# Moving the Vector engine's preparation of later weights from the projections of the first layer to the copies of its product stage

## The chip, the cores and the metric

The kernel runs on one core of a Trainium2 chip, in one launch. The metric is the device time of that launch in microseconds, median of several runs. One execution was profiled; all times inside the kernel are of that execution, counted from the start of its span. Engines are TensorE (PE, with its weight loads as PEld), the Vector engine (DVE), the Scalar engine (ACT), GpSimd (POOL) and SyncE (SP), which issues the DMAs.

## The reference, cut to what matters

The input `x` is an array of 128 x 128 positions with 32 channels. Eight layers follow each other, each added to its input. Four are mixers: a triangle product (L0), another (L1), a recurrent convolution over rows (SC) and a third triangle product (L3). Between them stand a top-k expert layer (F0), two sigmoid recurrences (R1 and R2) and a top-2 expert layer (F3). The change works in L0:

```
zn  = layernorm(x)
a   = sigmoid(zn @ Wga + bga) * (zn @ Wla + bla)
b   = sigmoid(zn @ Wgb + bgb) * (zn @ Wlb + blb)
k   = einsum('bimc,bmjc->bijc', a, b)          # per channel a 128 x 128 product
out = sigmoid(zn @ Wgo + bgo) * (layernorm(k) @ Wlo + blo)
x   = x + out
```

L1 and L3 have the same form, with the second operand of the product the other way round. The weights of L1, L3, F0, R1 and R2 must be scaled and laid out in blocks on the chip before their layers use them.

## The kernel before

All of `x` stays in on-chip memory. Its 128 x 4096 floats are worked on in 32 blocks `s` of 128 columns (4 rows of the picture by 32 channels), or in 8 batches `b` of 4 blocks. Each engine has its own program written out by hand, in order, and they meet on counting semaphores. DVE runs the layer norm of L0, then `tri_dve` for L0, then `f0_dve`, and so on.

A triangle layer goes through these stages:

- **Projection**, 32 blocks. TensorE multiplies block `s` by the projection weights (line 504) into one of four PSUM slots. ACT takes two sigmoids from the slot, `gate` (line 579) and `sig` (line 583). DVE multiplies the linear part by `sig` into `ab` (line 645) and signals `lin`. TensorE may not project block `s` before `lin` has been signalled for block `s - 4`, since it reuses that slot.
- **Turn**, L0 alone, 8 batches. TensorE transposes the second operand (line 364) into PSUM banks 0 and 1 in turn. ACT copies the even batches to `z_t` (line 372), DVE the odd ones (line 370). TensorE waits before batch `b` for the copy of batch `b - 2`.
- **Product**, 8 batches. TensorE makes the per-channel products (line 534) in four banks. ACT copies the even batches to `z` (line 573), DVE the odd ones (line 571, in `k_copy`). Before batch `b` of 4 or more TensorE waits for the copy of batch `b - 4`. The odd batches of the product also wait for DVE's copies of the turn, batch for batch.
- **Output**, 8 batches. When all product copies are done TensorE transposes `z` (line 555) and projects it (line 545). ACT squares, DVE sums, inverts and gates (lines 662, 668, 674), POOL scales and adds (lines 711, 716). The layer norm of the next layer is interleaved here.

While this goes on POOL copies weights of the convolution into `toep` (line 1209), and then forms the additive part of the output, two instructions for each of 8 batches (lines 621 and 630). It needs these before the output stage.

In L0's projection stage DVE also prepares weights of later layers, through the dictionary `between` of `tri_dve`, before blocks 4, 8, 12, 16 and 20:

- before blocks 4 and 8, `tri_weights1_dve` for L1 and L3: four instructions each (lines 451, 452, 453, 456);
- before blocks 12 and 16, `rec_weights1_dve` for R1 and R2: two instructions each (line 980), each from two operands in on-chip memory;
- before block 20, `f0_weights_dve`: two instructions (line 767).

TensorE reads the F0 weights when `f0_pe` begins, after all of L0, and the other four sets in `later_weights_pe`, in the middle of F0.

Of the kernel before, what the change touches and what calls it, by code (L numbers as in the profile page):

```python
# [107 lines left out]
def build(nc, x_d, par_d, row_d, mask_d, w1_d, w2_d, w2l_d, out_d):  # L108
    with ExitStack() as ctx:
# [47 lines left out]
        def bank(b, cols=BANK, n=1):  # L157
            return PSUM[:, b * BANK:b * BANK + (n - 1) * BANK + cols]
# [4 lines left out]
        def pcol(name, rows=GC):  # L163
            a, n = PAR[name]
            return par[0:rows, a:a + n]
# [48 lines left out]
        def wait_all(eng, levels):  # L214
            for s, v in levels:
                eng.wait_ge(s, v)

        t0 = stage("L0", "norm weights ones tri", "bt_ps bt_act bt_dve", src=XC, scratch=XR, eps=0, e2=EPS)
        f0 = stage("F0", "norm turn", "w_dve lg_ps lg_act pad best top neg cand_ps cand fin mk_ps mk sel exp esum tot_ps tot w wt_ps"
                   " wt_act wt_dve pool_ps pl plt_ps plt h_ps h o_ps outm_ps outm y_ps done", src=XC, eps=1, e2=0.0)  # L220
        t1 = stage("L1", "norm weights ones tri", "ab", src=XC, scratch=XR, eps=0, e2=EPS)
        r1 = stage("R1", "norm turn rec", "g_ps g_y0 g_y1 g_edge_ps g_edge g_turned", src=XC, eps=1, e2=0.0)
# [4 lines left out]
        r2 = stage("R2", "norm turn rec", "g_ps g_y0 g_y1 g_edge_ps g_edge g_turned", src=XC, eps=1, e2=0.0)  # L227
        t3 = stage("L3", "norm weights ones tri", src=XC, scratch=XR, eps=0, e2=EPS)
# [138 lines left out]
        def turn_copy(eng, L, b, dst, done, ps="zt_ps"):  # L367
            eng.wait_ge(L.s[ps], L.at[ps] + b + 1)
            if b % 2:
                eng.tensor_copy(dst, bank(b % 2)).then_inc(L.s[done], 1)  # L370
            else:
                eng.activation(dst, bank(b % 2), ACT.Copy).then_inc(L.s[done], 1)
# [76 lines left out]
        def tri_weights1_dve(dve, L):  # L449
            l, sm = L.name, L.s["w_half"]  # L450
            dve.tensor_scalar(scaled[l][:, :], pcol(f"{l}_w"), pcol(f"{l}_lnw"), None, ALU.mult).then_inc(sm, 1)
            dve.tensor_scalar(wotmp[l][:, GC:], pcol(f"{l}_wo"), pcol(f"{l}_low"), None, ALU.mult).then_inc(sm, 1)
            dve.tensor_scalar(lnb_at[l][:, :], last[:, :, :].rearrange("p g c -> p (g c)"), pcol(f"{l}_lnb", C), None,
                              ALU.mult).then_inc(sm, 1)
            dve.wait_ge(sm, L.at["w_half"] + 2)
            dve.tensor_tensor(wotmp[l][:, 0:GC].rearrange("p (g c) -> p g c", g=G),
                              wotmp[l][:, GC:].unsqueeze(1).to_broadcast([GC, G, C]),
                              m4[:, :].unsqueeze(2).to_broadcast([GC, G, C]), ALU.mult).then_inc(sm, 1)
# [106 lines left out]
        def k_copy(eng, L, b):  # L565

            eng.wait_ge(L.s["k_ps"], L.at["k_ps"] + b + 1)
            out = Z[:, :].rearrange("p (s g c) -> p c g s", g=G, c=C)[:, 4 * b:4 * b + 4]
            src = bank(KB[b % 4]).rearrange("p (c g s) -> p c g s", c=4, g=G)
            if b % 2:  # L570
                eng.tensor_copy(out, src).then_inc(L.s["k_dve"], 1)
            else:
                eng.activation(out, src, ACT.Copy).then_inc(L.s["k_act"], 1)
# [56 lines left out]
            eng.tensor_tensor(x, x, blocks(L.src)[:, :, 4 * b:4 * b + 4, :].rearrange("p g s c -> p s g c"), ALU.add)\  # L630
                .then_inc(L.s["xb"], 1)

        def tri_dve(dve, L, after, between={}):
            for s in range(S):
                if s in between:
                    between[s](dve)
                dve.wait_ge(L.s["sig"], L.at["sig"] + s + 1)
                sig = SIG[:, s % SLOTS, :].rearrange("p (h g w) -> p h g w", h=2, g=2)
                if L is t1:
                    if s >= 2:  # L640
                        dve.wait_ge(L.s["ab"], L.at["ab"] + s - 1)
                    dst = TMP[:, s % 2, 0:2 * GC].rearrange("p (h g w) -> p h g w", h=2, g=2)
                else:
                    dst = to_ab(s).rearrange("p (h g) w -> p h g w", h=2)
                dve.tensor_tensor(dst, slot(s)[:, :, :, 2 * C:4 * C], sig, ALU.mult).then_inc(L.s["lin"], 1)  # L645
                if L is t1 and s % 4 == 2 and s > 4:
                    gate_bias(dve, L, s // 4 - 1)
                    if s > 8:
                        add_x(dve, L, s // 4 - 2)
            if L is t1:  # L650
                gate_bias(dve, L, S // 4 - 1)
                add_x(dve, L, S // 4 - 2)
                add_x(dve, L, S // 4 - 1)
            if L is t0:
                for b in range(1, C // 4, 2):
                    turn_copy(dve, L, b, BT[:, 4 * b:4 * b + 4, :], "bt_dve", "bt_ps")
            for b in range(1, C // 4, 2):
                k_copy(dve, L, b)

            def out_sum(b):  # L660
                dve.wait_ge(L.s["o_sq"], L.at["o_sq"] + b + 1)
                dve.tensor_reduce(stats[:, 2, 16 * b:16 * b + 16],
                                  SQR[:, b * BANK:(b + 1) * BANK].rearrange("p (n c) -> p n c", c=C), AX.X, ALU.add)\
                    .then_inc(L.s["o_sum"], 1)

            def out_inverse(b):
                dve.wait_ge(L.s["o_std"], L.at["o_std"] + b + 1)
                dve.reciprocal(stats[:, 3, 16 * b:16 * b + 16], stats[:, 0, 16 * b:16 * b + 16]).then_inc(L.s["o_rstd"], 1)  # L668

            def out_gate(b):  # L670
                dve.wait_ge(L.s["o_rg"], L.at["o_rg"] + b + 1)
                if b >= 2:
                    dve.wait_ge(L.s["done"], L.at["done"] + b - 1)
                dve.tensor_tensor(TMP[:, b % 2, 0:BANK].rearrange("p (s h f) -> p h s f", s=4, h=2),  # L674
                                  o_bank(b)[:, :, :, 0, :],
                                  GATE[:, b * BANK:(b + 1) * BANK].rearrange("p (s h f) -> p h s f", s=4, h=2), ALU.mult)\
                    .then_inc(L.s["o_mul"], 1)

            for t in range(TRI_LN + LN_STEPS if after else S // 4 + 4):
                if 4 <= t < S // 4 + 4:  # L680
                    out_gate(t - 4)
                if 3 <= t < S // 4 + 3:
                    out_inverse(t - 3)
                if 2 <= t < S // 4 + 2:
                    out_sum(t - 2)
                if after:
                    ln_dve_step(dve, after, t - TRI_LN)
# [76 lines left out]
        def f0_weights_dve(dve):  # L764
            v = gw[:, :, :].rearrange("p q (b r e) -> p q b r e", b=G, r=2)
            for q in range(2):
                dve.tensor_tensor(v[:, q, :, q, :], pcol("gate").unsqueeze(1).to_broadcast([GC, G, E0]),
                                  m4[:, :].unsqueeze(2).to_broadcast([GC, G, E0]), ALU.mult).then_inc(f0.s["w_dve"], 1)
# [208 lines left out]
        def rec_weights1_dve(dve, L):  # L977
            W = rec_w[L.name]
            for name, key in (("W", "wbd"), ("VT", "vt")):
                dve.tensor_tensor(W[key][:, :].rearrange("p (g c) -> p g c", g=G),  # L980
                                  pcol(f"{L.name}_{name}").unsqueeze(1).to_broadcast([GC, G, C]),
                                  m4[:, :].unsqueeze(2).to_broadcast([GC, G, C]), ALU.mult).then_inc(L.s["w_half"], 1)
# [636 lines left out]
        @block.vector  # L1619
        def _(dve):  # L1620
            consts_dve(dve)
            ln_dve_step(dve, t0, 0)
            dve.wait_ge(par_first, PAR_FIRST)
            tri_weights1_dve(dve, t0)
            for u in range(1, LN_STEPS):
                ln_dve_step(dve, t0, u)
                if u == 1:
                    tri_weights2_dve(dve, t0)

            tri_dve(dve, t0, f0, {  # L1630
                4: lambda dve: tri_weights1_dve(dve, t1), 8: lambda dve: tri_weights1_dve(dve, t3), 12: lambda dve: rec_weights1_dve(dve, r1),
                16: lambda dve: rec_weights1_dve(dve, r2), 20: f0_weights_dve})
            f0_dve(dve)
            tri_dve(dve, t1, r1)
            rec_dve(dve, r1, None)
            turn_x_copy(dve, v1, 1)
            ln_dve(dve, sc)
            scan_dve(dve)
            turn_x_copy(dve, v2, 1)
            ln_dve(dve, r2)  # L1640
            rec_dve(dve, r2, t3)
            tri_dve(dve, t3, f3)
            f3_dve(dve)
# [73 lines left out]
```

## Time and profile before

| | |
|---|---|
| median of 3 runs | 615.32 us (614.03 to 616.44) |
| the profiled execution | 615.61 us |
| its span, first to last instruction | 613.8 us |
| PE busy | 455.4 us (74%) |
| DVE busy | 383.7 us (63%) |
| ACT busy | 237.9 us (39%) |
| POOL busy | 249.5 us (41%) |
| mean granted TensorE clock | 0.842 of full speed |
| chain that ended last | PE 54%, DVE 31%, ACT 6% |

The span and 1.81 us around it make the time of the profiled execution. L0's projection, turn and product stages lie between 28 and 64 us, less than a tenth of the span. The chain that ended last is followed back from the last instruction, step by step, to what released each instruction; only work on it can shorten the time.

### The profile page before, as it was taken

What the parts mean: (1) busy time and instruction counts of PE and PEld (TensorE: products, weight loads), DVE (VectorE), ACT (ScalarE), POOL (GpSimd) and SP (SyncE); (2) the same over time, 40 slices, a digit from 0 to 9 for tenths busy, and PEclk for the clock granted to TensorE, in tenths of its full rate; (3) what the DMA queues carried; (4) which work ended last, traced back from release to release, by engine and by line L of the source; (5) the groups of instructions that cost most, each with busy time, mean ns of one, the idle gap of its engine ahead of it and who ended that gap; (6) DMA issues with size and microseconds to landing.
All of it is one profiled execution on the core that took longest, in us unless ns stands there. A gap on an engine that the chain in (4) does not pass through costs nothing.

```text
span 613.8 us, 8600 instructions
## 1 busy us (share of the span) xinstructions
PE 455.4 (74%) x3018; PEld 356.4 (58%) x3018; DVE 383.7 (63%) x1148; ACT 237.9 (39%) x573; POOL 249.5 (41%) x325
## 2 busy tenths in 40 slices
PE   3788738798575854699658994879769854926996
PEld 2457634677342843399638994469636743914664
DVE  5796595535868487600792448920579489098885
ACT  1576534301465452457351003547449653200000
POOL 2795485000477078200050000500058478117995
PEclk9999967587789895989858999879859995557999
DMA  9100000000000000000000000000000000000323
GB/s 176 44 2 1 1 1 1 0 2 0 0 2 1 1 1 1 1 2 1 1 1 1 1 1 1 1 1 2 1 1 3 1 0 2 0 0 1 50 38 51
DMA packets 34105, 6.02 MB, mean 10 GB/s; under 512 B 33644, under 2 KB 33772, under 8 KB 34029
## 3 DMA queue, kind: packets, MB, share of 16 engines
q1 hardware_dynamic: 34062, 5.46, 5.1%
q8 instruction: 25, 0.41, 0.3%
q14 instruction: 18, 0.15, 0.1%
HBM read 3.36 MB, written 2.10 MB: 9 GB/s over the span
## 4 chain that ended last, share of the span: by engine, by line
PE 54%; DVE 31%; ACT 6%; issue 3%; POOL 3%; DMA 1%; SPq 1%; DVEq 0%; POOLq 0%
PE psum L1242 6%; DVE moments L290 6%; DVE ab L645 5%; PE psum L1003 5%; PE psum L504 5%; PE psum L384 5%; PE psum L1002 5%; DVE z L298 4%; PE psum L534 4%; PE psum L1415 3%; PE psum L545 3%; PE psum L1024 2%; PE psum L1393 2%; ACT z_t L319 2%; PE psum L1435 2%
## 5 line engine op out<-in xcount | busy, mean ns | idle before, releaser
L330 POOL TENSOR_TENSOR z<-z,stats 128x496 f32<-128x496 f32 (+1 forms) x64 | 67.0, 1047 | 136.6 <-DVE z L298 136.6
L384 PE MATMUL psum<-ident,z 128*128 128x128 f32 x256 | 57.6, 371 | 39.6 <-POOL z L330 38.4
L384 PEld LDWEIGHTS psum<-ident,z 128*128 128x128 f32 x256 | 41.3, 191 | 68.6 <-POOL z L330 48.3
L504 PE MATMUL psum<-wp_L,z_t 64*128 64x320 f32 x384 | 65.0, 477 | 11.1 <-DVE tmp L645 6.2
L319 ACT ACTIVATE z_t<-psum 128x512 f32<-128x512 f32 x56 | 40.1, 721 | 67.3 <-PE psum L384 67.3
L290 DVE BATCH_NORM_STATS2 moments<-x_cols 128x6 f32<-128x64 f32 x448 | 61.9, 210 | 2.1 <-POOL x_cols L716 1.7
L504 PEld LDWEIGHTS psum<-wp_L,z_t 64*128 64x128 f32 x384 | 37.3, 198 | 33.9 <-issue 27.4
L327 POOL MEMSET z<- 128x16 f32 x32 | 4.0, 125 | 128.1 <-DVE z L298 128.1
L1095 ACT ACTIVATE ab<-psum,mv 128x128 f32<-128x128 f32 x112 | 41.3, 369 | 19.9 <-PE psum L1003 9.5
L1003 PE MATMUL psum<-ab,R_vt 128*128 128x128 f32 x224 | 48.8, 302 | 0.0
L1002 PE MATMUL psum<-z_t,wbnt 128*128 128x128 f32 x224 | 46.6, 292 | 0.8 <-DVE wbnt L1148 0.8
L298 DVE TENSOR_TENSOR z<-x_cols,moments 128x496 f32<-128x496 f32 (+1 forms) x56 | 46.9, 838 | 0.0
L545 PE MATMUL psum<-wo_L,z_t 64*128 64x128 f32 x384 | 30.6, 303 | 20.7 <-DVE tmp L674 20.0
L711 POOL TENSOR_TENSOR gate<-gate,stats 128x512 f32<-128x512 f32 x24 | 25.1, 1048 | 45.4 <-DVE stats L668 45.2
L1522 POOL TENSOR_TENSOR z<-gate 128x512 f32<-128x512 f32 x31 | 38.7, 1267 | 7.0 <-DVE gate L1496 6.9
L1242 PE MATMUL psum<-ab,toep 128*128 128x128 f32 x336 | 39.4, 280 | 2.5 <-POOL ab L1225 1.6
L545 PEld LDWEIGHTS psum<-wo_L,z_t 64*128 64x128 f32 x384 | 26.2, 204 | 25.4 <-issue 14.2
L1242 PEld LDWEIGHTS psum<-ab,toep 128*128 128x128 f32 x336 | 39.1, 195 | 3.1 <-issue 3.1
L1496 DVE TENSOR_TENSOR gate<-psum,ab 128x1024 f32<-128x1024 f32 x32 | 37.8, 1219 | 4.4 <-PE psum L1420 3.3
L307 ACT ACTIVATE stats<-moments,eps 128x16 f32<-128x16 f32 x64 | 19.6, 307 | 50.1 <-DVE moments L290 50.1
L645 DVE TENSOR_TENSOR ab<-psum,sig 128x256 f32<-128x256 f32 x64 | 33.3, 604 | 7.8 <-ACT sig L583 7.8
L1002 PEld LDWEIGHTS psum<-z_t,wbnt 128*128 128x128 f32 x224 | 36.9, 207 | 1.4 <-DVE wbnt L1148 1.4
(244 smaller groups left out, 934.7 us busy)
## 6 DMA issues: line engine op xcount, KB each, us to landing
x_cols<-in_x_dram SPq DMA_DIRECT2D x16, 128.0 KB, 2.9
out_dram<-x_cols SPq DMA_DIRECT2D x32, 64.0 KB, 1.9
par<-in_par_dram SPq DMA_DIRECT2D x1, 644.5 KB
w<-in_w_dram SPq DMA_DIRECT2D x1, 264.0 KB
w<-in_w_dram SPq DMA_DIRECT2D x1, 256.0 KB
mask<-in_mask_dram SPq DMA_DIRECT2D x1, 64.0 KB
row<-in_row_dram SPq DMA_DIRECT2D x1, 3.3 KB
w2l<-in_w2l_dram SPq DMA_DIRECT2D x1, 2.0 KB
```

Source lines behind the costliest of these rows:

```text
L290: m = dve.bn_stats(moments[:, q, k:k + 2, :].rearrange("p k m -> p (k m)"), X4[:, SQ * q + s, g:g + 2, :].rearrange("p g c -> p c g"))
L298: dve.tensor_tensor(Z4[:, r, :, 0:c], X4[:, r, :, 0:c], ln_moment(before, 1).unsqueeze(3).to_broadcast([N, SQ, G, c]), ALU.subtract)\
L319: act.activation(dst, bank(q % 2).rearrange("p (s n) -> p s n", s=4), ACT.Copy).then_inc(L.s["zt"], 1)
L330: pool.tensor_tensor(Z4[:, r, :, 0:c], Z4[:, r, :, 0:c], RSTD[:, q].unsqueeze(3).to_broadcast([N, SQ, G, c]), ALU.mult).then_inc(L.s["z"], 1)
L384: m = pe.transpose(bank(b % 2)[:, k * N:(k + 1) * N], block_of(Z)(4 * b + k), ident[:, :])
L504: m = pe.matmul(bank(slot_bank(s) + h, 2 * 5 * C), ZT[rows, s, :], wp[l][rows, :, :], start=True, stop=True)
L545: m = pe.matmul(o_bank(b)[:, h, k, :, :], ZT[rows, 4 * b + k, :], wo[l][rows, :, rows], start=True, stop=True)
L645: dve.tensor_tensor(dst, slot(s)[:, :, :, 2 * C:4 * C], sig, ALU.mult).then_inc(L.s["lin"], 1)
L1002: return (pe.matmul(o, W["wbnt"][:, :], chunks(ZTIME, off, h), start=True, stop=False), lambda: pe.matmul(o, W["vt"][:, :], chunks(Y, off, ...
L1003: lambda: pe.matmul(o, W["vt"][:, :], chunks(Y, off, h), start=False, stop=True))
L1095: act.activation(chunks(Y, first + k + 1, h), bank(2 * h + k % 2, NS), ACT.Sigmoid, bias=bias).then_inc(L.s[f"step_y{h}"], 1)
L1242: m = pe.matmul(bank(2 + h, ROWS_S * NB), toep[:, b, :, :], scan_rows(SCN[:, :, b:b + NB], off, h), start=(b == 0), stop=(b == 2))
```

## The change

The dictionary goes, with its hook in the block loop. The same five calls are made later in L0's `tri_dve`, between the copies: L1's weights after the turn's copy 5, L3's after copy 7, R1's after the product's copy 1, R2's after its copy 3, F0's after its copy 7. The instructions are the same and in the same order among themselves. No wait and no semaphore is changed, no DMA is touched, and the other engines' programs stay as they are.

```diff
-        def tri_dve(dve, L, after, between={}):
+        def tri_dve(dve, L, after):
             for s in range(S):
-                if s in between:
-                    between[s](dve)
                 dve.wait_ge(L.s["sig"], L.at["sig"] + s + 1)
...
             if L is t0:
                 for b in range(1, C // 4, 2):
                     turn_copy(dve, L, b, BT[:, 4 * b:4 * b + 4, :], "bt_dve", "bt_ps")
+                    if b == 5:
+                        tri_weights1_dve(dve, t1)
+                tri_weights1_dve(dve, t3)
             for b in range(1, C // 4, 2):
                 k_copy(dve, L, b)
+                if L is t0 and b == 1:
+                    rec_weights1_dve(dve, r1)
+                if L is t0 and b == 3:
+                    rec_weights1_dve(dve, r2)
+            if L is t0:
+                f0_weights_dve(dve)
...
-            tri_dve(dve, t0, f0, {
-                4: lambda dve: tri_weights1_dve(dve, t1), 8: lambda dve: tri_weights1_dve(dve, t3), 12: lambda dve: rec_weights1_dve(dve, r1),
-                16: lambda dve: rec_weights1_dve(dve, r2), 20: f0_weights_dve})
+            tri_dve(dve, t0, f0)
```

## Rows read from the trace of the kernel before

**Rows 1.** Chain that ended last, L0: start us, us, engine, output, line.

```profile
29.09 1.94 DVE ab L645 x4
...
36.83 1.27 DVE R_vt L980
...
45.56 4.42 DVE ab L645 x8
...
55.44 7.16 PE psum L534 x64
62.63 1.02 DVE z L571
```

**Rows 2.** Timeline of DVE, L0's projection: start us, us, ..., idle before and releaser.

```profile
30.89 0.27 DVE L451 TENSOR_SCALAR scaled_L<-par 128x160 f32<-128x160 f32 x1
...
31.62 1.91 DVE L645 TENSOR_TENSOR ab<-psum,sig 128x256 f32<-128x256 f32 x4
...
35.92 0.92 DVE L980 TENSOR_TENSOR R_wbd<-par,m 128x128 f32<-128x128 f32 x1
36.76 1.35 DVE L980 TENSOR_TENSOR R_vt<-par,m 128x128 f32<-128x128 f32 x1
38.03 1.93 DVE L645 TENSOR_TENSOR ab<-psum,sig 128x256 f32<-128x256 f32 x4
39.80 0.88 DVE L980 TENSOR_TENSOR R_wbd<-par,m 128x128 f32<-128x128 f32 x1
40.61 0.28 DVE L980 TENSOR_TENSOR R_vt<-par,m 128x128 f32<-128x128 f32 x1
40.81 1.94 DVE L645 TENSOR_TENSOR ab<-psum,sig 128x256 f32<-128x256 f32 x4
42.60 0.87 DVE L767 TENSOR_TENSOR gw<-par,m 128x64 f32<-128x64 f32 x2
43.39 1.94 DVE L645 TENSOR_TENSOR ab<-psum,sig 128x256 f32<-128x256 f32 x4
45.56 4.41 DVE L645 TENSOR_TENSOR ab<-psum,sig 128x256 f32<-128x256 f32 x8 [0.23 <-ACT sig L583]
```

**Rows 3.** Timeline of DVE, L3's projection.

```profile
460.99 1.95 DVE L645 TENSOR_TENSOR ab<-psum,sig 128x256 f32<-128x256 f32 x4 [4.34 <-ACT sig L583]
463.16 15.36 DVE L645 TENSOR_TENSOR ab<-psum,sig 128x256 f32<-128x256 f32 x28 [0.21 <-ACT sig L583]
```

**Rows 4.** Timeline of PE, projections of L0 and L3 from block 4 on.

```profile
29.84 7.44 PE L504 MATMUL psum<-wp_L,z_t 64*128 64x320 f32 x48 [0.36 <-DVE ab L645]
...
461.73 15.58 PE L504 MATMUL psum<-wp_L,z_t 64*128 64x320 f32 x112 [0.35 <-DVE ab L645]
```

**Rows 5.** Timeline of DVE, L0's turn, product and start of output.

```profile
54.04 0.69 DVE L370 COPY z_t<-psum 128x512 f32<-128x512 f32 x1 [0.75 <-PE psum L364]
...
57.27 1.05 DVE L571 COPY z<-psum 128x512 f32<-128x512 f32 x1 [1.09 <-PE psum L534]
59.05 1.04 DVE L571 COPY z<-psum 128x512 f32<-128x512 f32 x1 [0.74 <-PE psum L534]
...
66.94 0.69 DVE L662 TENSOR_REDUCE stats<-squares 128x16 f32<-128x512 f32 x1 [3.30 <-ACT squares L594]
```

**Rows 6.** Timeline of POOL beside them.

```profile
36.64 1.31 POOL L621 TENSOR_TENSOR x_rows<-gate,bo_L 128x512 f32<-128x512 f32 x1
...
53.67 1.27 POOL L630 TENSOR_TENSOR x_rows<-x_rows,x_cols 128x512 f32<-128x512 f32 x1
```

**Rows 7.** Timeline of PE in F0, the same eight matmuls twice.

```profile
123.34 3.60 PE L801 MATMUL psum<-z,gate 128*128 128x256 f32 x8
...
127.21 1.89 PE L801 MATMUL psum<-z,gate 128*128 128x256 f32 x8
```

**Rows 8.** Stretches in F0: us, busy by engine, PEclk (granted clock), DMA.

```profile
124.00:125.00 1.00, 1.00 (x4) 0.82 (x3) 0.22 (x2) 0.00 (x0) 0.00 (x0) 0.50 0.00 0
...
127.00:128.00 1.00, 1.00 (x8) 0.92 (x7) 0.00 (x0) 0.59 (x1) 0.00 (x0) 1.00 0.00 0
```

## The prediction

> **What bounds the kernel now.** I read the page's shares first: TensorE is busy for 74% of the span, DVE for 63%. Those are means over unlike stages, so I went to the chain of waits in L0, where the change acts. The reader is to see in it [rows 1] that between 29.09 and 49.98 us nearly every piece is DVE's: multiplications of line 645, and between them weight instructions such as `R_vt`. So in this stage the weight instructions lie on the path that sets the end. Further on the chain goes to TensorE's products (line 534, 7.16 us) and then to DVE's last product copy.
>
> The second view is DVE's timeline over the same stretch [rows 2]. Four multiplications start to start take 1.80 us (29.09 in the chain [rows 1] to 30.89), or 0.45 each, and DVE has no idle time until 45.56, where it waits for ACT for the first time; from there eight take 4.41 us, 0.54 each. DVE alone could run at 0.45, something else at 0.54, and the weight work is what keeps DVE behind until just before 45.56.
>
> The third view is the same stage in L3, which has no weight work between its blocks [rows 3]. It is the same line, shape and count. There 32 multiplications go from 460.99 to 478.52, 17.53 us. TensorE's timeline says what sets that pace [rows 4]: its 112 records for 28 blocks fill 15.58 us with no wait shown inside, 0.556 a block, while in L0 the first 12 of these blocks (48 records) took 7.44 us and so 0.62 a block. So without the weights TensorE's projections and the loop over the four slots bound the stage, at L3's pace.
>
> **What is removed.** Fourteen instructions in five groups leave the projection stage. Start of the group to the multiplication behind it [rows 2]: L1's four 31.62 - 30.89 = 0.73, L3's four the same pattern, 0.73, R1's two 38.03 - 35.92 = 2.11, R2's two 40.81 - 39.80 = 1.01, F0's two 43.39 - 42.60 = 0.79. Sum 5.37 us. Check: 24 multiplications at 0.45 are 10.8; 29.09 + 10.8 + 5.37 = 45.3, where DVE does catch up. The saving is not 5.37, because TensorE then holds DVE back. I take the size from L3: L0's stage now takes 45.56 + 4.41 - 29.09 = 20.88 us, L3's 17.53. **Saving: 20.88 - 17.53 = 3.35 us.** The ends: at most 5.37 if nothing else held DVE, which L3 excludes; at least 3.0 if TensorE ran a little slower than in L3 (28 blocks at 0.567, which would add 0.3). I take 3.35: same instructions, and both stages run with POOL at work beside them.
>
> **What is added, group by group.** The turn and product stages move 3.35 us earlier as a whole; their inner gaps stay. I give the old times.
>
> L1's group goes behind the turn's copy 5, which starts at 54.04 and ends at 54.73. The copies there wait 0.75 us for TensorE each time [rows 5], and the group takes 0.73: hidden, with nothing to spare. What is queued behind it is copy 7. The product batch that reads copy 7 is the last one, and it starts at 55.44 + 7 x 0.895 = 61.7, so some 5 us of lateness would be borne there.
>
> L3's group goes behind copy 7. Before the first product copy DVE is idle for 1.09 us [rows 5]; the group takes 0.73: hidden, 0.36 to spare. Behind it is product copy 1, which TensorE needs at batch 5, at 55.44 + 5 x 0.895 = 59.9. The copy now ends at 58.32, so 1.6 us late costs nothing there.
>
> R1's and R2's groups go behind product copies 1 and 3, into gaps of 0.74 us [rows 5]. What they cost depends on POOL. In the projection stage the four instructions of line 980 took 0.92, 1.35, 0.88 and 0.28 us, all the same shape [rows 2]. The 1.35 us one starts at 36.76 and ends at 38.11; POOL's line 621 runs from 36.64 to 37.95 [rows 6], so it ended just behind POOL's. Undisturbed, the shape takes 0.28, and start to start 0.20 (40.61 to 40.81). Where are these groups against POOL? POOL is back to back and its schedule does not depend on this change; it ends at 53.67 + 1.27 = 54.94. R1's group now starts at 58.3 - 3.35 = 54.97. So it comes just as POOL ends: 0.40 us, hidden in 0.74. R2's is well clear. If R1's still took 2.11, copy 3 would start 1.37 late; TensorE needs it at batch 7 (61.7), it now ends at 60.09, so 1.6 us of cover remains, and the next gaps win 0.74 and more back.
>
> F0's group goes behind the last product copy. DVE then has 3.30 us idle [rows 5], against 0.79. TensorE wants these weights only after L0.
>
> The Trainium skill, "SBUF — State Buffer", section "Who interferes with whom", speaks against the change here: a Vector instruction with two on-chip inputs, or a `tensor_scalar` in a two-port mode, and a GpSimd instruction that reads the same memory exclude each other, and the later one fully blocks. The trace agrees for line 980 (1.35 us against 0.28). By the rule all eight instructions of the L1 and L3 groups, now moved from beside POOL's short `toep` copies to beside its long instructions, could each be held for one of these.
>
> Its price from rows: the first of these groups now starts at 54.73 - 3.35 = 51.4 and POOL runs to 54.9, so all the holds together are at most 3.5 us. Suppose DVE stands still until 54.9 and only then does the first group (0.73), copy 7 (0.69), the second group (0.73): these end at 57.1 and copy 1 at 58.1, where TensorE needs it at 59.9 - 3.35 = 56.55. TensorE stalls 1.5 us, and DVE, with 0.40 of R weights and 1.04 of copy in each 1.78 us from one copy's start to the next (57.27 to 59.05), follows again. So the added side costs **0 to 1.5 us**. I take 0: a hold of one POOL instruction (1.3 us) fits into 0.36 + 1.6.
>
> **Sum.** -3.35 + 0 = -3.35. The profiled execution, 613.8 span and 1.81 around it, would go from 615.61 to 612.26, the span to 610.45. That execution is 0.29 over the median of 615.32, so the median becomes **612.0 us** (-0.54%). POOL's end at 54.9 is no new bound: its next work is in the output stage, behind the last product copy, which starts at 62.63 and so at 59.28. Everything after L0 hangs on its end and on no DMA.
>
> **TensorE's clock** can add to it or take from it. The same eight matmuls of F0 take 3.60 us where the granted clock is 0.50 (1.2 GHz) and 1.89 where it is 1.00 (2.4 GHz) [rows 7, 8]. If a change of level falls one such batch earlier or later relative to the work, that is 1.7 us either way. I put nothing for it into the sum and use it for the range.
>
> **The rivals.** My forecast, 612.0, has 0.68; its own range is 610.3 to 613.7 by the 1.7 us.
>
> *POOL holds the moved groups.* As worked out: stall 1.5 us, gain 1.85, 613.5. For it is the 1.35 us row; against it the cover of 1.6 us. Chance 0.13.
>
> *The gain is given back or never comes.* L0 would not reach L3's pace, or the levels of TensorE's clock fall two batches of 1.7 us worse behind L0, which takes the whole 3.35: 615.3. For it: changes of level are there and F0 is bound by TensorE. Against: L3 shows the pace. Chance 0.11.
>
> *Faster still*: a clock change falls two batches better: 608.6. Chance 0.04.
>
> *Slower: the copies of the product become DVE's bound.* Twelve moved instructions stand ahead of the last product copy, on which the output stage waits. The idle time there is 0.75 + 1.09 + 3 x 0.74 = 4.06 us. If each were held as the worst row shows (1.35), they cost 16.2 - 4.06 = 12.1, net +8.8, 624.1. It decides the sign from a mean of (4.06 + 3.35) / 12 = 0.62 us an instruction, and is slower by over 0.5% from 0.87. Against it: POOL is done at 54.9, before the four R instructions, and no more than 3.5 us of holding is to be had. Chance 0.04.
>
> **How the numbers follow.** About 0.5% (3.08 us) is what a measurement of this kernel can tell from no change, so faster means below 612.24. My forecast lies 0.27 below that bound: of its 0.68 I count 0.41 as faster and 0.27 as the same. With 0.04 from the case faster still and 0.02 of the first rival (where the hold is short) that is 0.47 faster; slower is 0.04; the rest, 0.49, is the same. The range of 609.9 to 614.4 holds the forecast's own range and the first rival, 0.81, and leaves out the ends.
>
> **What would show it.** In the changed kernel's profile the multiplications of line 645 in L0 should stand without weight instructions between them and take 17.5 us, TensorE's 28 blocks 15.6. DVE's idle time before the copies should shrink from 0.75, 1.09 and 0.74 to about 0, 0.36 and 0.34, and that before the first `squares` sum from 3.30 to about 2.5. TensorE's products should still take 7.16 us with no wait for DVE. The R1 instructions should take 0.28 each. The prediction is wrong if product copies 1 or 7 start late and the chain runs over weight instructions again, or if the output stage starts 3.35 us earlier but the end does not: then the clock's stretches will have changed.

## The result and the profile after

The changed kernel takes 612.5 us (median of 12 runs, 611.12 to 614.04), the kernel before 615.85 us in the runs made beside it (614.03 to 617.55). The ratio is 0.9946, with a 95% interval of 0.9931 to 0.996: 0.54% less, 3.35 us. The forecast was 612.0 us and -0.54%. The profiled execution took 612.13 us with a span of 610.4, where the sum had 612.26 and 610.45.

DVE's timeline through L0, rows as in [rows 2] and [rows 5]:

```profile
29.23 1.95 DVE L643 TENSOR_TENSOR ab<-psum,sig 128x256 f32<-128x256 f32 x4 [3.06 <-ACT sig L583]
31.39 15.34 DVE L643 TENSOR_TENSOR ab<-psum,sig 128x256 f32<-128x256 f32 x28 [0.22 <-ACT sig L583]
...
50.80 0.69 DVE L370 COPY z_t<-psum 128x512 f32<-128x512 f32 x1 [0.75 <-PE psum L364]
51.41 0.46 DVE L451 TENSOR_SCALAR scaled_L<-par 128x160 f32<-128x160 f32 x1
51.79 1.25 DVE L452 TENSOR_SCALAR wotmp_L<-par 128x32 f32<-128x32 f32 x1
...
53.35 0.67 DVE L370 COPY z_t<-psum 128x512 f32<-128x512 f32 x1
53.95 0.71 DVE L451 TENSOR_SCALAR scaled_L<-par 128x160 f32<-128x160 f32 x1
...
55.13 1.03 DVE L571 COPY z<-psum 128x512 f32<-128x512 f32 x1
56.01 0.27 DVE L987 TENSOR_TENSOR R_wbd<-par,m 128x128 f32<-128x128 f32 x1
...
56.40 1.02 DVE L571 COPY z<-psum 128x512 f32<-128x512 f32 x1
...
59.38 1.01 DVE L571 COPY z<-psum 128x512 f32<-128x512 f32 x1 [0.69 <-PE psum L534]
60.25 0.33 DVE L774 TENSOR_TENSOR gw<-par,m 128x64 f32<-128x64 f32 x2
63.69 0.69 DVE L669 TENSOR_REDUCE stats<-squares 128x16 f32<-128x512 f32 x1 [3.11 <-ACT squares L594]
```

The multiplications now stand together, from 29.23 to 46.73: 17.50 us, where they took 20.88 [rows 1, 2] and L3's take 17.53 [rows 3]. The moved groups fill the time in which DVE waited for TensorE. Two instructions stand out, at 51.79 and 53.95, far longer than their like before. In the kernel before the one of line 452 was

```profile
31.08 0.23 DVE L452 TENSOR_SCALAR wotmp_L<-par 128x32 f32<-128x32 f32 x1
```

and the one of line 451 took 0.27 us [rows 2].

TensorE's timeline of the same stages, to be read beside [rows 4]:

```profile
29.96 15.55 PE L504 MATMUL psum<-wp_L,z_t 64*128 64x320 f32 x112 [0.35 <-DVE ab L643]
...
52.03 7.31 PE L534 MATMUL psum<-ab,z_t 128*128 128x128 f32 x64
60.54 1.06 PE L555 MATMUL psum<-ident,z 128*128 128x128 f32 x8 [1.20 <-DVE z L571]
```

Its 28 blocks run without a wait (15.55 us), its products too (7.31, as before), and the output stage begins 1.20 us after them. Before the change the wait was the same 1.20 us, and the stage began at 63.79, 3.25 us later:

```profile
63.79 1.06 PE L555 MATMUL psum<-ident,z 128*128 128x128 f32 x8 [1.20 <-DVE z L571]
```

From the start of the output stage to the end of the span it is 550.0 us before (613.8 - 63.79) and 549.9 after (610.4 - 60.54), so in these two executions nothing behind L0's product stage changed. POOL's timeline:

```profile
51.72 1.28 POOL L621 TENSOR_TENSOR x_rows<-gate,bo_L 128x512 f32<-128x512 f32 x1
53.08 1.48 POOL L630 TENSOR_TENSOR x_rows<-x_rows,x_cols 128x512 f32<-128x512 f32 x1
```

The chain that ended last, in order of time, has no weight instruction between the first multiplication and the output stage:

```profile
31.39 15.35 DVE ab L643 x28
...
50.80 0.70 DVE z_t L370
...
52.20 7.16 PE psum L534 x64
...
59.38 1.02 DVE z L571
```

### The profile page after: what moved, and what is told of

Read it like the earlier page. It is cut to its first block, busy times and chain, and to the rows that moved or that the text cites. A ratio compares the mean times of both kernels' runs of the same rounds, so it can differ in the third digit from the quotient of the medians.

```text
span 610.4 us, 8600 instructions
## 1 busy us (share of the span) xinstructions
PE 453.6 (74%) x3018; PEld 354.2 (58%) x3018; DVE 384.0 (63%) x1148; ACT 237.5 (39%) x573; POOL 249.0 (41%) x325
## 4 chain that ended last, share of the span: by engine, by line
PE 54%; DVE 31%; ACT 6%; issue 3%; POOL 3%; DMA 1%; SPq 1%; DVEq 0%; POOLq 0%
PE psum L1249 6%; DVE moments L290 6%; DVE ab L643 5%; PE psum L1010 5%; PE psum L1009 5%; PE psum L384 5%; DVE z L298 4%; PE psum L504 4%; PE psum L534 4%; PE psum L1422 3%; PE psum L545 3%; PE psum L1031 2%; PE psum L1400 2%; ACT z_t L319 2%; PE psum L1442 2%
## 5 line engine op out<-in xcount | busy, mean ns | idle before, releaser
L504 PEld LDWEIGHTS psum<-wp_L,z_t 64*128 64x128 f32 x384 | 35.6, 197 | 32.2 <-issue 27.3
L643 DVE TENSOR_TENSOR ab<-psum,sig 128x256 f32<-128x256 f32 x64 | 34.6, 607 | 7.8 <-ACT sig L583 7.8
```

The costliest lines, as they stand in the source:

```text
L504: m = pe.matmul(bank(slot_bank(s) + h, 2 * 5 * C), ZT[rows, s, :], wp[l][rows, :, :], start=True, stop=True)
```

## The experiments

Unless said otherwise each median is of 10 to 12 runs, and the kernel before ran beside them: 615.69 us for the first four, 616.42 for the next ones. Their intervals are 0.32% to 0.51% wide, so a time is good to about 1 us, and stage lengths are taken from profiles. Outside of the stages at issue the executions differ by as much: in the 13 profiles the first multiplication starts between 28.2 and 29.2 us, and from the start of L0's output stage to the end it is 549.2 to 550.8 us, in one case 551.9. In 5 of the 13 profiles of this study (with those of before and after) TensorE's granted clock is 0.50, that is 1.2 GHz, for some 3 us from about 29 or 30 us. Here is that stretch in the first experiment, windows with granted clock third from the end:

```profile
26.00:30.00 4.00, 2.93 (x15) 1.48 (x15) 1.41 (x4) 3.03 (x11) 3.88 (x20) 0.81 0.01 2
30.00:31.00 1.00, 1.00 (x6) 0.74 (x4) 0.53 (x2) 0.20 (x2) 0.94 (x7) 0.50 0.00 0
```

A projection stage with this stretch is compared only with another such.

**All five groups behind the last product copy.**

```diff
             for b in range(1, C // 4, 2):
                 k_copy(dve, L, b)
...
             if L is t0:
+                tri_weights1_dve(dve, t1)
+                tri_weights1_dve(dve, t3)
+                rec_weights1_dve(dve, r1)
+                rec_weights1_dve(dve, r2)
                 f0_weights_dve(dve)
```

> The changed kernel with all five weight groups behind the last product copy, where DVE is idle 3.11 us in the changed kernel; unheld they need 0.73 + 0.73 + 0.40 + 0.40 + 0.2 = 2.5 us. Theory (in the changed kernel the copies that start up to 1.2 us late are fully covered by the four product banks): product copies now start on time, and nothing is gained: output stage starts as long after the first multiplication as in the changed kernel (31.3 us), median within 0.3 us of its 612.5. Rival (the late copies or POOL's 1.48 us instruction cost something hidden): faster than the changed kernel by 0.5 to 1.5 us.

Measured: 612.48 us, ratio 0.9947 (0.9929 to 0.9965), the same as the changed kernel. DVE's timeline:

```profile
54.68 1.04 DVE L571 COPY z<-psum 128x512 f32<-128x512 f32 x1 [1.10 <-PE psum L534]
56.46 1.04 DVE L571 COPY z<-psum 128x512 f32<-128x512 f32 x1 [0.74 <-PE psum L534]
...
64.35 0.69 DVE L666 TENSOR_REDUCE stats<-squares 128x16 f32<-128x512 f32 x1 [0.81 <-ACT squares L594]
```

The copies are on time, all groups fit before the first sum of squares with 0.81 us to spare, and nothing is gained by it. So the late copies of the changed kernel cost nothing that these runs can tell. (From first multiplication to output stage it takes 32.6 us and not 31.3, because this profile has the stretch at 1.2 GHz: its projection stage is 18.79 us long.)

**L1's and L3's groups back in the projection.**

```diff
             for s in range(S):
+                if L is t0 and s == 4:
+                    tri_weights1_dve(dve, t1)
+                if L is t0 and s == 8:
+                    tri_weights1_dve(dve, t3)
                 dve.wait_ge(L.s["sig"], L.at["sig"] + s + 1)
...
-                    if b == 5:
-                        tri_weights1_dve(dve, t1)
-                tri_weights1_dve(dve, t3)
```

> The changed kernel with the L1 and L3 groups (four instructions each) back before blocks 4 and 8 of the projection; the R1, R2 and F0 groups stay moved. Theory (TensorE loses what DVE is late beyond the slots' slack): in the kernel before TensorE's first 12 waiting blocks took 7.44 us, 0.77 more than at L3's pace, so these two groups cost 0.8 us of their 1.46; projection stage 18.3 us, median 613.3. Rival A (their debt is paid back in full by DVE's surplus of 0.1 us a block): 17.5 us, 612.5. Rival B (each us of DVE work costs a us): 19.0 us, 614.0.

Measured: 613.39 us, ratio 0.9957 (0.9938 to 0.9975). The median is where the theory has it, 0.9 over the changed kernel, but rival B's 614.0 is not excluded by it. The profile has the stretch at 1.2 GHz, and its stage, 29.10 to 49.95, takes 20.85 us. Against the 18.79 of the first experiment, which has that stretch too, this is 2.06 us more, where the theory had 0.8 and rival B 1.5. In this execution one instruction of a group was held:

```profile
35.39 1.29 DVE L453 TENSOR_SCALAR lnb_at_L<-last,par 32x128 f32<-32x128 f32 x1
```

This had been 0.27 us in the kernel before, so about 1 of the 2.06 us is this hold. What the two groups cost in the stage at full clock no run shows. POOL's line 630 stands beside it:

```profile
35.30 1.30 POOL L630 TENSOR_TENSOR x_rows<-x_rows,x_cols 128x512 f32<-128x512 f32 x1
```

**The kernel before, with POOL late.** Only POOL's start on the additive part is moved, so that no long POOL instruction runs beside a weight group. The weight groups stay in the projection.

```diff
                 pool.wait_ge(L.s["w_dve"], L.at["w_dve"] + TRI_W)
+                if L is t0:
+                    pool.wait_ge(L.s["lin"], L.at["lin"] + 22)
                 for b in range(S // 4):
                     gate_bias(pool, L, b)
```

> The kernel before, weight groups inside the projection, but POOL starts its additive part of L0's output only after 22 of the 32 multiplications, so none of its long instructions runs beside a weight group. POOL then ends near 62 us, before the output stage needs it. Theory (more than half of the 5.37 us of the groups was DVE held by POOL): the line 980 instructions take 0.28 us each, the groups sum to about 2.5 us, the projection stage takes 18.4 us (20.9 before), median 613.3. Rival (the price is the count of the instructions, the holds matter little): stage 20.2 us or more, median 615.2. Rival (line 980 is slow for another reason, such as fetching its code): it stays at 0.9 to 1.35 us.

Measured: 612.94 us, ratio 0.9936 (0.9915 to 0.9956): POOL's start alone is worth what the change is worth, as far as the runs can tell (the two medians differ by 2.75 us, which is at the edge of that interval). The first profile has the stretch at 1.2 GHz and a stage of 20.03 us, 1.24 over the first experiment's 18.79. A second profile of the same kernel:

> The kernel before with POOL's late start once more, for a profile: in the first one TensorE's granted clock was 0.50 from about 30 to 33 us, which lengthened the projection stage (20.0 us). Theory: where the clock stays at 1.00 in that stretch the stage takes 18.4 us. Rival (the groups still cost nearly what they did): 20 us at full clock too.

One execution, 612.91 us, with full clock throughout the stage. DVE's timeline, beside [rows 2]:

```profile
35.89 0.26 DVE L982 TENSOR_TENSOR R_wbd<-par,m 128x128 f32<-128x128 f32 x1
36.08 0.27 DVE L982 TENSOR_TENSOR R_vt<-par,m 128x128 f32<-128x128 f32 x1
36.28 2.22 DVE L645 TENSOR_TENSOR ab<-psum,sig 128x256 f32<-128x256 f32 x4
...
40.53 0.34 DVE L769 TENSOR_TENSOR gw<-par,m 128x64 f32<-128x64 f32 x2
40.91 6.59 DVE L645 TENSOR_TENSOR ab<-psum,sig 128x256 f32<-128x256 f32 x12
```

Line 980's instructions (here 982) take 0.26 to 0.28 us, R1's group 0.39 and not 2.11. The stage runs from 29.08 to 40.91 + 6.59 = 47.50: 18.42 us, as expected; neither rival has that. The five groups now take 2.65 us together (0.74, 0.75, 0.39, 0.39 and 0.38), in place of 5.37. So of the 3.38 us that the weights cost in the projection, 20.88 - 18.42 = 2.46 were POOL's holds, and 18.42 - 17.50 = 0.92 is what was left of the groups' own 2.65.

**The changed kernel, with POOL late.** The same edit in the changed kernel.

> The changed kernel with POOL's start as late as in the run above: POOL now runs beside all of the turn and product stages. It ends near 62 us, and the output stage needs it at 66. Theory (POOL holds DVE instructions with two on-chip inputs and tensor_scalar; the cover of the product copies is finite, some 1.6 us to TensorE's batches 5 and 7, and none behind the last copy): R1's and R2's groups are held too (1 to 2 us each instead of 0.4), product copy 3 starts over 2 us late, TensorE stalls and the last copy is late: slower than the changed kernel by 0.5 to 2.5 us. Rival (holds are absorbed whatever they are): same as the changed kernel, last copy on time.

Measured: 615.63 us, ratio 0.9998 (0.998 to 1.0016): the whole gain is gone, 3.1 us, more than the 0.5 to 2.5 expected. DVE's timeline:

```profile
53.64 1.25 DVE L452 TENSOR_SCALAR wotmp_L<-par 128x32 f32<-128x32 f32 x1
...
56.08 0.49 DVE L989 TENSOR_TENSOR R_wbd<-par,m 128x128 f32<-128x128 f32 x1
56.49 1.35 DVE L989 TENSOR_TENSOR R_vt<-par,m 128x128 f32<-128x128 f32 x1
57.77 1.03 DVE L571 COPY z<-psum 128x512 f32<-128x512 f32 x1
58.65 0.54 DVE L989 TENSOR_TENSOR R_wbd<-par,m 128x128 f32<-128x128 f32 x1
59.11 1.36 DVE L989 TENSOR_TENSOR R_vt<-par,m 128x128 f32<-128x128 f32 x1
60.39 1.88 DVE L571 COPY z<-psum 128x512 f32<-128x512 f32 x2
```

and TensorE's:

```profile
56.37 2.02 PE L534 MATMUL psum<-ab,z_t 128*128 128x128 f32 x16 [0.78 <-DVE z L571]
58.94 1.13 PE L534 MATMUL psum<-ab,z_t 128*128 128x128 f32 x8 [0.55 <-DVE z L571]
62.42 1.06 PE L555 MATMUL psum<-ident,z 128*128 128x128 f32 x8 [2.35 <-DVE z L571]
63.73 2.08 PE L545 MATMUL psum<-wo_L,z_t 64*128 64x128 f32 x16 [0.25 <-ACT z_t L605]
```

The projection stage is as short as in the changed kernel (17.49 us). But all four of R1's and R2's instructions are held now, TensorE waits 0.78 and 0.55 for copies 1 and 3, and 2.35 for the last, in place of 1.20. The output stage starts 62.42 - 28.16 = 34.26 us after the first multiplication, against 31.31: 2.95 later. After these waits the granted clock falls to 0.50 (1.2 GHz) shortly before 64 us, which the expectation did not count: the first output projection takes 2.08 us, not 1.16, and the first sum of squares comes 38.33 us after the first multiplication, 3.87 later than in the changed kernel.

**R1's and R2's groups back in the projection.**

```diff
             for s in range(S):
+                if L is t0 and s == 12:
+                    rec_weights1_dve(dve, r1)
+                if L is t0 and s == 16:
+                    rec_weights1_dve(dve, r2)
                 dve.wait_ge(L.s["sig"], L.at["sig"] + s + 1)
...
-                if L is t0 and b == 1:
-                    rec_weights1_dve(dve, r1)
-                if L is t0 and b == 3:
-                    rec_weights1_dve(dve, r2)
```

> The changed kernel with the R1 and R2 groups (two instructions of line 980 each) back before blocks 12 and 16 of the projection, POOL at its usual place; the L1, L3 and F0 groups stay moved. Theory (POOL's holds make these four instructions the dear ones: 2.11 and 1.01 us in the kernel before, where TensorE then waited 1.48 and 0.37): projection stage about 19.5 us, median 614.5, 2.0 over the changed kernel, dearer than the eight instructions of the L1 and L3 groups were (0.9). Rival (price goes by count and length, 4 x 0.20 = 0.8 us, most of it absorbed): stage 17.7, median 612.7.

Measured: 613.64 us, ratio 0.9958 (0.9942 to 0.9974). That is 2.8 under the kernel before and so some 0.6 over the changed one, not 2.0; the rival's figure is nearer. Its profile has the stretch at 1.2 GHz, and the four instructions took 0.49, 0.28, 0.81 and 0.28 us. A second profile of the same kernel:

> R1 and R2 groups inside the projection, once more for a profile. In the first profile their four instructions took 0.49, 0.28, 0.81 and 0.28 us, 1.56 us start to next multiplication for both groups, not 3.12. Theory (how long POOL holds them depends on where in a POOL instruction they come, and that moves with the stretch of granted clock 0.50 near 30 us): without that stretch the groups cost another sum, above 2 us, and the stage takes over 18.5 us. Rival (they cost 1.6 us wherever nothing was late before them): again 1.5 to 1.7.

One execution, full clock in the stage:

```profile
35.43 0.74 DVE L987 TENSOR_TENSOR R_wbd<-par,m 128x128 f32<-128x128 f32 x1
36.09 1.35 DVE L987 TENSOR_TENSOR R_vt<-par,m 128x128 f32<-128x128 f32 x1
37.36 1.93 DVE L647 TENSOR_TENSOR ab<-psum,sig 128x256 f32<-128x256 f32 x4
39.15 0.88 DVE L987 TENSOR_TENSOR R_wbd<-par,m 128x128 f32<-128x128 f32 x1
...
42.31 6.60 DVE L647 TENSOR_TENSOR ab<-psum,sig 128x256 f32<-128x256 f32 x12 [0.22 <-ACT sig L583]
```

The groups take 1.93 and 1.00 us and the stage 42.31 + 6.60 - 28.99 = 19.92, 2.42 over the changed kernel. In the execution with the slower stretch it took 20.12 against 18.79 in the first experiment, 1.33 over. The mechanism is as the theory has it; its size goes by the execution, and the median shows less of it (some 0.6) than either profile does. Why the median shows so little stays open. In the execution with the slower stretch the stage is 2.62 us longer than in the changed kernel's profile and the whole only 1.43 (613.56 against 612.13): it started its multiplications 0.81 us sooner and took 0.4 us less behind the product stage.

**A load behind product copy 5, and the same behind copy 7.** Ten instructions whose result nobody reads are added, into a new tile `spare`, with `b == 5` in one kernel and `b == 7` in the other:

```diff
                 if L is t0 and b == 3:
                     rec_weights1_dve(dve, r2)
+                if L is t0 and b == 5:
+                    for k in range(10):
+                        dve.tensor_tensor(spare[:, k, :], cent[:, :], ident[:, :], ALU.mult)
```

> The changed kernel with ten extra instructions that nobody reads (128x128, two on-chip inputs, 0.20 us each, 2.0 in all) behind product copy 5 of L0, when POOL is idle. Theory (the last product copy is the one without cover): DVE ends copy 5 at 58.55 and the load at 60.55, copy 7 was due at 59.38, so it is 1.2 late and so is everything behind it: median 613.7. Rival (the wait on the last copy is hidden by ACT's copy or the output's fill): within 0.3 of 612.5.

> The same ten extra instructions behind product copy 7, where DVE is idle 3.11 us in the changed kernel. Theory: hidden, the first sum of squares is on time, median 612.5. Rival (any DVE work in L0 costs its length): 614.5.

Measured, beside 616.42 for the kernel before: 614.20 us (ratio 0.9959, 0.9943 to 0.9976) behind copy 5, and 613.25 us (7 runs, ratio 0.9932, 0.9906 to 0.9957) behind copy 7. Taken as differences to the kernel before on the same chip these are -2.2 and -3.2, against the changed kernel's -3.35: by the medians the load costs 1.1 us in the one place and next to nothing in the other. The intervals overlap, so the profiles have to carry this. DVE's and TensorE's rows for the load behind copy 5:

```profile
58.24 2.08 DVE L667 TENSOR_TENSOR spare<-cent,ident 128x128 f32<-128x128 f32 x10
60.25 0.99 DVE L572 COPY z<-psum 128x512 f32<-128x512 f32 x1
...
61.39 1.92 PE L556 MATMUL psum<-ident,z 128*128 128x128 f32 x8 [2.31 <-DVE z L572]
```

TensorE waits 2.31 us for the last copy in place of 1.20, which is 1.11 more. In this execution more is lost behind it, for the granted clock (third from the end) falls:

```profile
62.00:63.00 1.00, 1.00 (x7) 0.90 (x5) 0.00 (x0) 0.51 (x1) 0.00 (x0) 0.50 0.00 0
```

The eight transposes take 1.92 us, not 1.06, and the first sum of squares comes 36.89 us after the first multiplication, 2.43 later than in the changed kernel. Behind copy 7 the load leaves the first sum of squares 1.10 us to spare:

```profile
61.38 2.08 DVE L667 TENSOR_TENSOR spare<-cent,ident 128x128 f32<-128x128 f32 x10
...
64.83 0.69 DVE L673 TENSOR_REDUCE stats<-squares 128x16 f32<-128x512 f32 x1 [1.10 <-ACT squares L595]
```

**The kernel before, profiled twice more**, to see whether its holds are chance.

> The kernel before, unchanged, once more for a profile. Theory: the four line 980 instructions and the two of line 767 vary between 0.28 and 1.35 us with POOL's phase; at full clock the stage takes 20 to 21.5 us, with a stretch at clock 0.50 near 30 us more of the loss lies there and less in DVE's lateness. Rival (fixed lengths, not set by phase): 0.92, 1.35, 0.88, 0.28 again.

> The same, a second time: how often the stretch at clock 0.50 near 30 us comes, and whether the lengths follow it.

Two executions, 614.85 and 614.39 us, both with full clock in the stage. From the first:

```profile
35.71 0.91 DVE L980 TENSOR_TENSOR R_wbd<-par,m 128x128 f32<-128x128 f32 x1
36.55 1.35 DVE L980 TENSOR_TENSOR R_vt<-par,m 128x128 f32<-128x128 f32 x1
```

The second has 0.93 and 1.35 for these, and F0's pair takes 0.88 and 0.89. So the lengths of [rows 2] came back within 0.02 us, against the theory: in all three profiles at full clock DVE and POOL fall into the same step. The stage takes 20.95 and 20.96 us. The rival of fixed lengths has the numbers right for this kernel, but POOL late and the same instructions at 0.27 us show that POOL sets them.

## Why the prediction was right

- **The saving in the projection** was taken from L3, 20.88 - 17.53 = 3.35 us. Measured: 20.88 - 17.50 = 3.38, at 15.55 us for TensorE's 28 blocks (15.58 in L3). The other profiles at full clock agree: 20.95 and 20.96 for the kernel before, 17.49 and 17.54 for two kernels without weights in the projection. That the medians moved by just 3.35 us as well is closer than the runs can tell: their interval goes from 2.5 to 4.2 us. The choice of a later stage of the same kernel as the model, and not of the sum of the removed instructions (5.37), is what made the number. It holds for executions at full clock; none of the kernel before with the slower stretch was profiled, so the stage's saving in those is open.
- **L1's and L3's groups** were costed at 0.73 us each and took 1.94 (51.41 to 53.35) and 1.18 (53.95 to 55.13), because POOL held them. The forecast had named that and bounded the holds at 3.5 us; they were 1.66 together. Its expected idle times of DVE (0, 0.36 and 0.34) were therefore wrong: there is none before product copies 1, 3 and 5. One half of its own sign of being wrong did come, a late copy 1; the other half, weight instructions on the chain, did not.
- **The cover** was right. Against the spacing of before, shifted by the 3.25 us between the two starts of the output stage (63.79 and 60.54), copy 1 started 1.1 us late and copy 3 0.6; copy 5 was back to 0.1 and copy 7 on time. The 1.6 us of slack at TensorE's batches 5 and 7 was not used up (copy 1 ended at 56.16, and 0.5 us of it was left), and the kernel with everything behind the last copy is no faster.
- **R1's group** was to start at 54.97 and POOL to end at 54.94, a margin of 0.03 us on which up to 2.11 - 0.40 = 1.71 us of holding hung. It was not so close: POOL ended at 54.56 and the group started at 56.01, and its two instructions took 0.27 each. Both times were forecast wrongly and both errors helped. The group came late because the groups ahead of it had been held. POOL's schedule, said not to depend on the change, ended 0.38 sooner: it began its long instructions 0.19 us sooner and was held less (before, one took 1.53 us at 33.81 and one 1.41 at 40.61; in the changed kernel these take 1.27 or 1.28, and one at 53.08 takes 1.48). F0's group took 0.33 us and not 0.79, so DVE's idle time behind it is 3.11 us and not about 2.5.
- **The slower rival** was right in kind and named the right point, the last product copy: 1.2 us of lateness put there made TensorE wait 1.11 us longer, and the median 1.1 us longer. The first rival's mechanism, POOL's holds, is real too, and with POOL's work moved over the product stage it takes the entire gain. What decides is when POOL ends. In the changed kernel that is 54.56, 0.6 us before product copy 1.
- **TensorE's clock** added nothing between the two profiled executions: the start of the output stage moved by 3.25 us, and what follows it takes 550.0 and 549.9. Over many executions it can't be told from the rest within the interval.
- What was not seen: why the weight groups were so dear. The sum named R1's held instruction, but took 5.37 us as the groups' price. 2.46 of the 3.38 us lost were POOL's doing, by the one profile at full clock with POOL late. A change of one wait on POOL, without moving any DVE work, gave the same time within what these runs can tell (0.9936, 0.9915 to 0.9956, against 0.9946). I found no version that beats the changed kernel beyond the measurement.

## What to carry to other kernels

If the same stage stands elsewhere in the kernel without the extra work, its length is the first estimate of what remains, and the gain of moving the work is the difference of the two stages, not the sum of the instructions. Here this was right to 0.03 us where the sum was 2 us too high. When you move work into gaps, look for the one instruction behind which there is no buffer (here the last copy): lateness ahead of it is paid back over the buffers as long as it is smaller than their slack (1.1 us against 1.6 here, and too much with POOL late), lateness at it is paid in full. And before moving DVE instructions with two on-chip operands, or `tensor_scalar`, look at what POOL does beside them, for it may be cheaper to move POOL.

## What the runs showed of the hardware

- A DVE instruction that comes while one of POOL's long instructions runs is held and ends just behind it (0.04 to 0.16 us), whatever its own size: 128x32 elements took 1.25 us and 128x128 took 1.35, against 0.23 and 0.27 alone, while POOL's took 1.27 to 1.31. This hit `tensor_scalar` with one tensor input as well as `tensor_tensor` with two, and none of the copies from PSUM (0.67 to 0.69 us with and without POOL). POOL is held as well, by less: where its instruction began while one of DVE's was running, it took up to 1.53 us and not 1.27 (at 33.81 in the kernel before, beside DVE's at 33.72 and 33.92, which took 0.27 each; 1.48 at 53.08 in the changed kernel). So of a group of small instructions only some are held. The Trainium skill, "SBUF — State Buffer", section "Who interferes with whom", has it that the first to issue keeps the shared ports and the other blocks, for a Vector instruction with two on-chip inputs and for `tensor_scalar` in a two-port mode. The trace agrees that either engine can be the one that waits. In which mode these `tensor_scalar` ran no profile shows, and the starts do not always tell who was first: the one of DVE's at 33.92 began 0.11 us behind POOL's and was not held.
- In 5 of 13 profiles TensorE's clock was at 1.2 GHz for about 3 us at the head of L0's projection, in the other 8 at 2.4. It goes by the execution: two of the kernels (the one before with POOL late, and the one with R1's and R2's groups back) were profiled twice, once with it and once without. It made the stage 1.3 us longer (18.79 against 17.50). That this is part of the 3 us by which runs of one kernel differ is likely and was not measured.
